# Two mixtures of experts in one program: both in parts of 8, 12, 8 and 4 groups, with the scatters and gathers queued anew

## What is computed

```python
x = x + 0.5 * moe_gelu(layernorm(x))      # layer 2; after it layer 3:
x = x + 0.5 * moe_swiglu(layernorm(x))

def moe(x):                               # 8 experts, each token goes to the best 2
    top2 = top_k(x @ gate_w, 2)
    g = softmax over the two chosen
    gelu:   h = gelu(x @ w1[e] + b1[e]);           y = h @ w2[e] + b2[e]     # 128 -> 512 -> 128
    swiglu: h = silu(x @ w1[e]) * (x @ w3[e]);     y = h @ w2[e]             # 128 -> 256 -> 128
    out = sum over the two experts of g * y;       gelu: out = layernorm(out) * ln_g + ln_b
```

## Time and profile before

| | |
|---|---|
| median of 3 runs | 1292.12 us (1291.59 to 1297.62) |
| the profiled execution | 1289.35 us, its span 1287.6 us |
| busy in the span | PE 1006.0, DVE 877.7, POOL 746.8, ACT 599.5 us |
| TensorE's mean granted clock | 0.908 of full speed |
| the joint program | about 349 to 816 us |

### The profile page before, as it was taken

The page is one execution under the profiler, slowest core; times in us unless marked ns, Lnnn a source line. Parts: engine busy times, 40 slices in busy tenths (PEclk is TensorE's granted clock), DMA queues, the critical chain, the costliest instruction groups (busy, mean ns, idle before and its releaser), DMA issues. The chain is left out here.

```text
span 1287.6 us, 28074 instructions
## 1 busy us (share of the span) xinstructions
PE 1006.0 (78%) x6835; PEld 849.4 (66%) x6836; DVE 877.7 (68%) x3115; ACT 599.5 (47%) x1746; POOL 746.8 (58%) x721
## 2 busy tenths in 40 slices
PE   2599999477466999978788794598789874599893
PEld 2499999444255999978787794244344444589892
DVE  5655678577783666786577564689969967466763
ACT  0256777556323667755344353351345131245562
POOL 2787458720047566775757666266635734767555
PEclk9999999787858999999899897799999985799997
DMA  7745345200012333322233342000000000334353
GB/s 233 229 135 135 105 138 150 67 1 0 0 48 72 101 100 93 105 83 86 93 102 93 99 132 80 6 1 1 0 1 0 0 0 17 95 112 127 102 148 108
DMA packets 146194, 102.92 MB, mean 80 GB/s; under 512 B 16324, under 2 KB 134934, under 8 KB 146070
## 3 DMA queue, kind: packets, MB, share of 16 engines
q1 hardware_dynamic: 70530, 39.35, 10.6%
q0 software_dynamic: 16384, 33.59, 8.7%
q10 hardware_dynamic: 59156, 28.57, 7.6%
HBM read 52.44 MB, written 49.02 MB: 79 GB/s over the span
## 5 line engine op out<-in xcount | busy, mean ns | idle before, releaser
L595 PE MATMUL gelu_hb<-gelu_xsT,gelu_weights 128*128 128x128 f32 x2208 | 303.8, 283 | 2.5 <-issue 2.5
L595 PEld LDWEIGHTS gelu_hb<-gelu_xsT,gelu_weights 128*128 128x128 f32 x2208 | 279.9, 199 | 3.0 <-issue 2.7
L692 ACT ACTIVATE gelu_hid<-gelu_hb,gelu_weights 128x128 f32<-128x128 f32 x736 | 209.1, 375 | 122.2 <-PE gelu_hb L595 90.4
L1232 POOL DMA_INDIRECT slots_x<-gelu_xn,gelu_index x176 | 175.4, 996 | 94.4 <-issue 45.7
L606 PE MATMUL gelu_ob<-w,gelu_hid 128*128 x1472 | 196.4, 277 | 3.9 <-DVE gelu_ys L974 3.5
L606 PEld LDWEIGHTS gelu_ob<-w,gelu_hid 128*128 128x128 f32 x1472 | 180.5, 194 | 5.2 <-issue 5.2
L986 DVE COPY gelu_weights<-w 128x516 f32 x184 | 87.0, 490 | 64.5 <-issue 35.2
L1908 POOL TENSOR_TENSOR rwkv_tw<-rwkv_tw,rwkv_qr 128x512 f32<-128x512 f32 x64 | 79.5, 1273 | 54.0 <-DVE rwkv_tw L1867 44.9
L595 PE MATMUL swiglu_hb<-swiglu_xsT,swiglu_weights 128*128 128x128 f32 x736 | 100.3, 281 | 0.0
L974 DVE TENSOR_TENSOR gelu_ys<-gelu_ob,bias 128x128 f32<-128x128 f32 x184 | 49.5, 287 | 71.1 <-PE gelu_ob L606 68.1
L595 PEld LDWEIGHTS swiglu_hb<-swiglu_xsT,swiglu_weights 128*128 128x128 f32 x736 | 92.3, 198 | 0.0
(11 more groups left out here) (382 smaller groups left out, 2108.6 us busy)
## 6 DMA issues: line engine op xcount, KB each, us to landing
gelu_xs<-slots_x SPq DMA_DIRECT2D x69, 256.0 KB
slots_y<-gelu_ys ACTq DMA_DIRECT2D x138, 128.0 KB
swiglu_xs<-slots_x SPq DMA_DIRECT2D x23, 256.0 KB
slots_y<-swiglu_ys ACTq DMA_DIRECT2D x46, 128.0 KB
raw_s<-in_L_ffn_w ACTq DMA_DIRECT2D x12, 256.0 KB
slots_x<-zeros SPq DMA_DIRECT2D x2, 1472.0 KB, 10.4
slots_x<-gelu_xn,gelu_index POOLq DMA_INDIRECT x176, 2.4
w<-in_L_ffn_w SPq DMA_DIRECT2D x1, 2048.0 KB, 13.8
```

The source lines that it names most:

```text
L595: last = pe.matmul(hb[j][:, c * P:(c + 1) * P], weights[:, odd * BODY + j, c * P:(c + 1) * P], xsT[j // SET][:, j % SET, :], start=True, s ...
L692: last = act.activation(hid[:, j % RING, c * P:(c + 1) * P], hb[j][:, c * P:(c + 1) * P], ACT.Gelu, bias=weights[:, odd * BODY + j, FF + c ...
L1232: pool.indirect_dma_start(slots_x[:, :], bass.IndirectOffsetOnAxis(index[p][:, k, g:g + 1], 0), tokens[p][:, g, :], None).then_inc(sent[p] ...
```

## The change

The GELU parts of the joint program get 8, 12, 8, 4 groups, the same as the SwiGLU parts, so a SwiGLU part takes its tokens from the same groups of `x` and `xn` as the GELU part before it. The buffers for gathered results (`back`) and the small routing buffers (`DRAWER`) are laid out anew, equal for both stages. The GELU parts begin at tiles 0, 23, 54, 77; the SwiGLU parts stay at 92, 115, 146, 169. All the side work of the joint program gets new places in the four tables and in GpSimd's list. Part 4 (8 groups) is scattered between the gathers of part 1 and of part 2; part 5 (12 groups) after both gathers of part 2 and before those of part 3; part 6 is scattered around the norm of part 3. The eight waits for `sent` go (in three places), four waits for `combined` come. The change in the diff, cut to its core (in the tables, only DVE's and the rows of the others that are spoken of):

```diff
-PARTS_OF = {..., ("gelu", "swiglu"): ((4, 12, 8, 8), (8, 12, 8, 4))}
+PARTS_OF = {..., ("gelu", "swiglu"): ((8, 12, 8, 4), (8, 12, 8, 4))}
...
         if both:
-            tokens += [of(apart, 0, behind), of(xn, GROUP0[2], behind + 1),
-                       of(xn, 0, behind + 2), of(xn, PART_GROUPS[behind + 2], behind + 3)]
+            tokens += tokens
...
-        DRAWER = [0, 1, 2, 3, 1, 2, 1, 3][:NPARTS]
+        DRAWER = [p % PARTS for p in ALL]
...
         if both:
-            back += [halves(xn, PART_GROUPS[behind], GROUP0[2]), beside_xn(behind + 1), halves(apart, PART_GROUPS[behind + 2]),
-                     halves(small, PART_GROUPS[behind + 3])]
+            one, other = spare
+            narrow = [t[:, PART_GROUPS[1]:PART_GROUPS[1] + PART_GROUPS[3], :] for t in (other, apart)]
+            back = [halves(one, PART_GROUPS[0]), [of(t, 0, 1) for t in (other, apart)], halves(one, PART_GROUPS[2]), narrow] * 2
...
 TensorE's table
-                                           21: {1: at(turn_tokens, 5, 0), 2: at(turn_tokens, 5, 1), 3: at(turn_tokens, 5, 2)},
-                                           22: {0: at(logits, 5, 0) + at(logits, 5, 1) + at(logits, 5, 2), 3: at(count_tokens, 5)},
+                                           13: {3: at(turn_tokens, 4, 0)},
+                                           14: {0: at(turn_tokens, 4, 1), 2: at(logits, 4, 0) + at(logits, 4, 1)},
+                                           22: {2: at(turn_tokens, 5, 0), 3: at(turn_tokens, 5, 1)},
+                                           23: {0: at(turn_tokens, 5, 2), 2: at(logits, 5, 0) + at(logits, 5, 1) + at(logits, 5, 2)},
+                                           24: {3: at(count_tokens, 5)},
...
 DVE's table
-                                           17: {0: at(combine, 1, 1) + at(norm, 1, 1), 3: at(route, 4)},
-                                           18: {0: at(finish, 1, 1), 1: at(places, 4), 3: at(combine, 1, 2) + at(norm, 1, 2)},
-                                           19: {0: at(table, 4), 2: at(combine, 2, 0) + at(norm, 2, 0)},
-                                           20: {1: at(finish, 1, 2), 2: at(finish, 2, 0), 3: at(stats, 5)},
-                                           21: {0: at(normalise, 5)},
-                                           22: {1: at(route, 5)},
-                                           23: {0: at(places, 5), 2: at(table, 5), 3: at(combine, 2, 1) + at(norm, 2, 1)},
-                                           24: {1: at(gates, 4)},
-                                           25: {2: at(finish, 2, 1)},
-                                           28: {2: at(gates, 5)},
-                                           29: {0: at(combine, 3, 0) + at(norm, 3, 0)},
-                                           30: {1: at(combine, 3, 1) + at(norm, 3, 1), 3: at(finish, 3, 0)},
-                                           31: {0: at(stats, 6), 1: at(finish, 3, 1), 3: at(normalise, 6)},
-                                           32: {1: at(stats, 7), 3: at(route, 6)},
-                                           33: {1: at(normalise, 7), 2: at(places, 6), 3: at(combine, 4, 0)},
-                                           34: {0: at(table, 6), 2: at(combine, 4, 1), 3: at(route, 7)},
+                                           9: {2: at(combine, 0, 0), 3: at(norm, 0, 0)},
+                                           10: {2: at(combine, 0, 1), 3: at(norm, 0, 1)},
+                                           12: {0: at(finish, 0, 0), 1: at(finish, 0, 1), 3: at(stats, 4)},
+                                           13: {2: at(normalise, 4)},
+                                           15: {0: at(route, 4)},
+                                           16: {1: at(places, 4)},
+                                           17: {2: at(combine, 1, 0), 3: at(norm, 1, 0)},
+                                           18: {3: at(combine, 1, 1)},
+                                           19: {0: at(norm, 1, 1), 2: at(finish, 1, 0), 3: at(table, 4)},
+                                           20: {0: at(combine, 1, 2), 1: at(norm, 1, 2), 2: at(finish, 1, 1)},
+                                           21: {0: at(finish, 1, 2), 1: at(stats, 5)},
+                                           22: {0: at(normalise, 5)},
+                                           24: {0: at(route, 5), 2: at(gates, 2)},
+                                           25: {0: at(places, 5), 2: at(table, 5)},
+                                           26: {0: at(combine, 2, 0), 1: at(norm, 2, 0)},
+                                           27: {0: at(combine, 2, 1) + at(norm, 2, 1) + at(gates, 3),
+                                                1: at(finish, 2, 0) + at(finish, 2, 1) + at(stats, 6) + at(normalise, 6) + at(route, 6)},
+                                           28: {1: at(places, 6), 3: at(table, 6)},
+                                           29: {1: at(gates, 4)},
+                                           30: {0: at(combine, 3, 0), 1: at(norm, 3, 0)},
+                                           31: {2: at(finish, 3, 0), 3: at(stats, 7)},
+                                           32: {1: at(gates, 5)},
+                                           33: {0: at(normalise, 7)},
+                                           34: {2: at(route, 7)},
+                                           35: {0: at(gates, 6), 2: at(places, 7)},
                                            36: {0: at(table, 7)},
+                                           37: {0: at(combine, 4, 0)},
+                                           38: {2: at(combine, 4, 1)},
...
 GpSimd's list
-            send(1, after=(-2, 2) if both else at_tile(0))
+            send(1, after=at_tile(0))
...
+            if both:
+                final_power(0, 0)
+                final_power(0, 1)
+                power(4)
             await_sets(-(-TILE0[2] // SET))
             if both:
-                final_power(0, 0)
-                fetch(1, 0, after=at_tile(55))
...
-                for p in range(PARTS):
-                    pool.wait_ge(sent[p], SENT[p])
...
+                fetch(1, 0, after=at_tile(58))
+                fetch(1, 1, after=at_tile(63))
                 final_power(1, 0)
+                fetch(1, 2, choices=[0], after=at_tile(69))
                 final_power(1, 1)
+                fetch(1, 2, choices=[1], after=at_tile(71))
+                send(4, range(0, 3), after=at_tile(75))
+                final_power(1, 2)
+                send(4, range(3, 7), after=at_tile(79))
+                power(5)
+                send(4, range(7, 8), after=at_tile(84))
+                gate_power(4)
+                pool.wait_ge(combined, QUAD0[1])
                 await_sets(-(-TILE0[3] // SET))
+                fetch(2, 0, after=at_tile(86))
+                fetch(2, 1, after=at_tile(92, 2))
+                send(5, range(0, 5), after=at_tile(102, 1))
                 final_power(2, 0)
                 final_power(2, 1)
+                send(5, range(5, 9), after=at_tile(104, 1))
+                power(6)
+                send(5, range(9, 12), after=at_tile(105, 1))
                 gate_power(5)
                 await_sets(TILE0[4] // SET)
+                fetch(3, 0, after=at_tile(106, 1))
+                send(6, range(0, 4), after=at_tile(112, 3))
                 final_power(3, 0)
+                send(6, range(4, 8), after=at_tile(118, 3))
+                gate_power(6)
+                pool.wait_ge(combined, QUAD0[3])
                 await_sets(-(-TILE0[5] // SET))
                 power(7)
+                fetch(4, 0, after=at_tile(126, 3))
+                fetch(4, 1, after=at_tile(133, 3))
+                send(7, after=at_tile(144, 2))
                 gate_power(7)
                 await_sets(-(-TILE0[6] // SET))
                 for q in range(QUADS[5]):
                     fetch(5, q, after=at_tile(148 + 6 * q, 3))
+                pool.wait_ge(combined, QUAD0[5])
                 await_sets(-(-TILE0[7] // SET))
+                fetch(6, 0, after=at_tile(170, 3))
                 fetch(6, 1)
+                pool.wait_ge(combined, QUAD0[4])
```

112 lines of the change are left out of this document (39 added, 73 removed).

## The result

The changed kernel takes 1287.5 us (median of 7 runs, 1286.6 to 1289.5), the kernel before 1292.8 beside it (7 runs, 1291.6 to 1297.7): ratio 0.9955, interval 0.9937 to 0.9973. That is a gain of 5.2 us, 0.4%, where 13 were forecast. It is inside the forecast's range and has its sign, but only 0.4 of its size.

What follows compares the result with a forecast made beforehand. TensorE was busiest but uneven, stalling for scattered rows, and GpSimd's launches set the joint program's end. Terms +14.7, -17.5, -6.2, +20.6, -13.1 and -11.5 gave -13.0 us off the 1292.12 median: 1279, range 1264 to 1294.

Steps and rivals of the forecast that it cites:

- The start: Before iteration 0 of the joint program: 8 groups in part 0, not 4, put it at 393.1 us, 14.7 later.
- The step that the first mixture gives the whole stage: Start of the GELU stage: the first mixture, set 337.8 us later, puts iteration 12 at 489.8 us, before 492.6.
- The middle of the GELU stage: Iterations 12 to 23: part 1's stores awaited until 509.9 us, part 4's load at 584.9, iteration 23 at 590.
- gain 9 to iteration 23: Iteration 23 starts at 590 us, before 599.0: a gain of 9, bounds 5 to 13.
- Part 5: Iterations 23 to 28: index ready at 614 us, last scatter at 649.3, iteration 28 at 656.5, 11.6 behind.
- costs nothing beyond this: DVE's long block in iteration 27, about 20 us, adds nothing while TensorE awaits scatters; without that cover up to 15.
- What comes back: From iteration 28: 28 to 35 takes 49 us, not 62.1; no stall at 36; last gather 793.4, before 806.4.
- rival C: Iterations 28 to 35 stay at 62.1 us, DVE being slowed by TensorE's restarts: no gain, 1292; chance 0.18.
- B: Smaller DVE loss: iterations 23 and 24 take 7.5 us, 28 to 35 takes 45; 21 gained, 1271; chance 0.20.
- D: In GpSimd's queue `final_power(2, 1)` awaits a late norm ahead of 14 scatters: end 20 us later, 1299; chance 0.13.
- E: DVE's weight copies prolong each of GpSimd's 176 launches by 0.5 us: +88 on the forecast, 1367; chance 0.01.

## Why the prediction was right in sign and wrong in size

Times in us; the forecast's mark, then the measured one. First the forecast's own sum, each term the change in the distance to the kernel before:

| term | forecast | measured |
|---|---|---|
| start, to iteration 0 | +14.7 | +16.6 |
| to iteration 12 | -17.5 | -18.8 |
| to iteration 23 | -6.2 | -0.8 |
| to iteration 28 | +20.6 | +22.6 |
| to iteration 35 | -13.1 | -11.4 |
| to the last gather | -11.5 | -11.7 |
| sum | -13.0 | -3.6 |

- **The start.** First scatter 367.2, measured 369.0; iteration 0 at 393.1, measured 395.0. Iteration 12 at 489.8, measured 490.3. The step that the first mixture gives the whole stage is right; the stall before iteration 3 is gone.
- **The middle of the GELU stage: the step that failed.** Load of part 4 at 584.9, measured 591.0. The first gather was put at 509.9 and came at 514.2: the wait for part 1's stores ended at 512.5, 2.6 later than forecast, and an addition stands between, which the forecast had left out there. From there to the first scatter 46.9 us were allotted and 48.1 taken, but not for the reasons given: the launches, additions and powers are 39.5 us, and two waits for the norms of part 1, 5.1 and 3.5 us, make up the rest. The forecast had no wait for `final_power(1, 0)` and `final_power(1, 1)` at all, and had priced six additions and two powers too high: its sum leaves 16.4 us for them beside 24 launches, and they took 9. That these two errors nearly cancel is luck. The waits were what could be won back: 8 to 10 us of time came once scatters filled them and a power stood behind. The miss of 6.1 us at the load is made up of the later first gather (4.3), 1.2 from there to the first scatter, and 0.6 over part 4's scatters and the way to the load. The term "gain 9 to iteration 23" measured 3.0 (598.96 to 595.95).
- **Part 5.** Iteration 23 to index 24 forecast, 26 measured; the index at 622.0, not 614. Scatters 35.3 forecast, 36.0 measured. 4.1 us from the last scatter to the load, as forecast, and iteration 28 at 664.6, not 656.5: 19.6 behind the kernel before, not 11.6. That DVE's block "costs nothing beyond this" is true by 0.4 us.
- **What comes back.** 28 to 35 in 50.6, 49 forecast, 62.1 before. This step is right, and rival C with it wrong. No stall at 36 (7.1 us from 35, 6.2 forecast, 18.1 before). From 36 to the last gather 80.6, 81.6 forecast.
- **Sum.** Last gather out at 802.8, forecast 793.4, before 806.4: 3.6 of 13.0 us. The 9.4 us missing are 6.0 before iteration 23, 2.1 from there to the index (12 groups of routing took 26 us, not 24), and 1.4 from the index on. From the last gather to the end the profiled execution took 1.7 us more than before's, so its span gained 1.9; the medians say 5.2.
- **The rivals.** B did not occur: iterations 23 and 24 took 10.0 and 8.5 us, not 7.5. D did not: `final_power(2, 1)` waited 1.2 us. E did not: the changed kernel's 256 scatters took 0.96 to 1.39 us, median 0.96; 60 of them ran beside one of DVE's weight copies, and their median is 0.97, the longest 1.39. What the forecast never considered is the other direction, GpSimd's wide additions holding DVE up.

## What to carry to other kernels

Where one engine issues all transfers from a fixed list, write down for each wait in the list when it will be met, not only the sum of the list: the idle time before a wait is the cheapest place for launches that are already possible, and here six of them, with one power moved behind, were worth 8 to 10 us on one kind of chip. But count who waits for what is pushed back by it. And measure an order of instructions on more than one chip before calling a change of half a per cent a gain.

## What the hardware showed that was not expected

- A GpSimd addition of 128x512 fp32 holds up DVE's instructions, and is hardly held up itself (1.27 to 1.38 us each in the row of four, 1.26 to 1.36 elsewhere): a DVE pair of products took 0.43 alone and 1.50 beside it, a copy of 128x516 0.43 and 1.00, and a DVE operation on 128x4, 0.17 us elsewhere, took 1.44 and ended with the addition. In one execution this cost TensorE 4 to 5 us. Powers of 128x12 on GpSimd, 9 us of them in the wait for part 5's index, cost the kernel nothing on the first kind of chip; they did not stand beside the same DVE instructions. The Trainium skill (SBUF — State Buffer, Who interferes with whom) says that a DVE instruction with two SBUF inputs contends with a GpSimd instruction that reads SBUF; the pair of products agrees. The price in the end time stays open.
- Chips differ by 19 to 20% on this program, and by the sign of a change of half a per cent. In the stretches read, part of the excess is idle time with nothing named: TensorE's instructions 1.1 us apart that the other kind of chip runs back to back.
